# Second attention of a two-layer block: maxima over two PSUM banks at once, exponentials one bank at a time

## What is computed

```python
x = x + _L0_xattn_ref(_layernorm(x), ...)       # one head, 256 wide
x = x + _L0_ffn_ref(_layernorm(x), ...)         # 16 routed experts (top 2), 2 shared
x = x + _L1_xattn_ref(_layernorm(x), ctx, ...)  # 16 heads of 16, 4 key heads, over the 256 channels
x = x + _L1_ffn_ref(_layernorm(x), ...)         # ternary weights, 1024 wide
```

```python
q = q * cos + _rotate_half(q) * sin
k = k * cos + _rotate_half(k) * sin
k = jnp.repeat(k, 4, axis=1); v = jnp.repeat(v, 4, axis=1)
scores = jnp.einsum('bhqd,bhkd->bhqk', q, k) * scale
attn = jax.nn.softmax(scores, axis=-1)
out = jnp.einsum('bhqk,bhkd->bhqd', attn, v)
```

## Time and profile before

| | us |
|---|---|
| median of 3 runs | 815.56 (814.92 to 822.73) |
| the profiled execution, its own time | 824.98 |
| its span, first to last instruction | 823.2 |
| TensorE busy | 569.1 (69% of the span) |
| VectorE busy | 465.4 (57%) |
| ScalarE busy | 328.3 (40%) |
| GpSimd busy | 255.4 (31%) |
| maxima, 256 of 128x512 | 163.7 |
| exponentials, 128 of 128x1024 | 128.2 |

### The profile page before, as it was taken

How to read it: one execution, slowest core, us unless ns; L and a number is a source line. 1 busy time by engine, 2 the same in 40 slices (tenths; PEclk the granted TensorE clock), 3 DMA queues, 4 the chain that set the end, 5 groups by cost and what they waited for, 6 DMA issues and landing times. The chain is left out here.

```text
span 823.2 us, 11743 instructions
## 1 busy us (share of the span) xinstructions
PE 569.1 (69%) x4241; PEld 330.9 (40%) x4241; DVE 465.4 (57%) x1011; ACT 328.3 (40%) x488; POOL 255.4 (31%) x312
## 2 busy tenths in 40 slices
PE   3797907784882976633256877768876887776977
PEld 1575704674651756632022223223432342222444
DVE  2347660747831677752585686746766765660332
ACT  1113117455310656420023443524564546555523
POOL 2003125555374000035546122454323230000513
PEclk9898957986965989885557567879898998787979
DMA  9932082133124578522605210451115210101100
GB/s 259 299 109 87 26 268 73 36 77 106 39 103 127 130 194 199 122 89 30 118 1 117 53 31 22 91 106 17 39 29 115 39 41 2 31 6 26 29 26 26
DMA packets 97012, 68.73 MB, mean 83 GB/s; under 512 B 44265, under 2 KB 91003, under 8 KB 95995
## 3 DMA queue, kind: packets, MB, share of 16 engines
q1 hardware_dynamic: 91403, 56.18, 28.3%
q0 software_dynamic: 3504, 11.54, 4.8%
q10 hardware_dynamic: 2048, 0.27, 0.2%
HBM read 31.00 MB, written 24.38 MB: 67 GB/s over the span
## 5 line engine op out<-in xcount | busy, mean ns | idle before, releaser
L1773 DVE TENSOR_REDUCE M<-ps 128x2 f32<-128x512 f32 x256 | 163.7, 682 | 83.6 <-PE ps L1069 83.2
L1006 ACT ACTIVATE RW<-ps 128x1024 f32<-128x1024 f32 x128 | 128.2, 1024 | 138.8 <-PE ps L1069 126.4
L1069 PE MATMUL ps<-RS 128*128 128x128 f16 (+3 forms) x912 | 95.1, 270 | 40.9 <-DVE RS L1667 16.5
L1069 PEld LDWEIGHTS ps<-RS 128*128 128x128 f16 (+1 forms) x912 | 83.1, 130 | 53.1 <-DVE RS L1667 18.5
L1069 PE MATMUL ps<-RW,Vs 128*32 128x256 f32 x1024 | 89.8, 482 | 10.5 <-ACT wqkvo L1018 9.4
L1069 PE MATMUL ps<-RS,RW 48*128 48x256 bf16 (+1 forms) x448 | 58.6, 315 | 17.5 <-DVE M L1773 14.1
L1069 PE MATMUL ps<-tmp,xrow 48*128 48x256 bf16 x256 | 31.8, 334 | 40.9 <-DVE M L1773 25.5
L890 POOL TENSOR_TENSOR RS<-RS,RW 128x512 f16<-128x512 f32 x32 | 36.6, 1155 | 68.7 <-ACT RW L1054 68.7
L1069 PE MATMUL ps<-RS,wqkvo 128*128 128x512 f32 x64 | 36.5, 728 | 23.5 <-ACT RS L907 23.5
L1069 PE MATMUL ps<-RW,RS 50*128 50x512 bf16 (+1 forms) x224 | 45.0, 405 | 11.0 <-DMA RW<-mlo 8.9
L1069 PEld LDWEIGHTS ps<-RW,Vs 128*32 128x32 f32 x1024 | 31.1, 128 | 49.1 <-issue 24.5
(11 more groups left out here) (220 smaller groups left out, 964.3 us busy)
## 6 DMA issues: line engine op xcount, KB each, us to landing
sorted_scratch<-zero SPq DMA_DIRECT2D x1, 6144.0 KB, 19.9
expert_scratch<-RS SPq DMA_DIRECT2D x24, 256.0 KB, 2.7
RW<-in_wg SPq DMA_DIRECT2D x6, 384.0 KB, 6.2
RW<-in_wu SPq DMA_DIRECT2D x6, 384.0 KB, 6.6
RW<-in_w SPq DMA_DIRECT2D x3, 768.0 KB, 7.3
q_scratch<-RS SPq DMA_DIRECT2D x12, 192.0 KB, 2.7
acc<-in_x SPq DMA_DIRECT2D x4, 512.0 KB, 7.6
RS<-in_ctxT SPq DMA_DIRECT2D x8, 256.0 KB, 4.1
```

What stands on the lines that cost most here:

```text
L1006: act.activation(PT[:, k, :, :].rearrange("p i k -> p (i k)"), tile("st", n, 2), ACT.Exp, scale=float(HD) ** -0.5)\
L1069: return pe.matmul(out, lhsT, rhs, start=first, stop=last)
L1773: dve.tensor_reduce(M[:, 2 * p + kv // 2, at:at + 2], tile("smax", 2 * n + i).rearrange("p (a b) -> p a b", a=2), AX.X, ALU.max).then_inc( ...
```

## The change

The ring `max` gets a fourth bank, and a `smax` tile is now the two banks of a whole piece: four matmuls write it, one semaphore tells it full, and one reduction takes the maxima of both samples (1024 columns, four results a partition). `q1`, `mt` and `o1` now also take two banks of this ring, though they fill one at most. The ring `st` has three banks, and a `st` tile is one bank: two tiles a piece, each with its own wait for room, its own signal and its own exponential of 512 columns. `xt4`, `up4`, `gate4` and `down4` stay at one bank each, in a ring of three. The other lines follow the new counts.

```diff
-RINGS = {"main": (0, 1, 2, 3, 4, 5, 6), "max": (0, 1, 2), "st": (3, 4, 5, 6), "pv": (7,)}
+RINGS = {"main": (0, 1, 2, 3, 4, 5, 6), "max": (0, 1, 2, 3), "st": (4, 5, 6), "pv": (7,)}
...
     if what == "q1":
-        return [("q1", n, "max", 1, 2)]
+        return [("q1", n, "max", 2, 2)]
     if what == "mt":
-        return [("mt", n, "max", 1, 2)]
+        return [("mt", n, "max", 2, 2)]
     if what == "max":
-        return [("smax", m, "max", 1, 1) for m in two]
+        return [("smax", n, "max", 2, 1)]
     if what == "st":
-        return [("st", n, "st", 2, 1)]
+        return [("st", m, "st", 1, 1) for m in two]
...
     if what == "o1":
-        return [("o1", n, "max", 1, 1)]
+        return [("o1", n, "max", 2, 1)]
...
             def st(n):
-                act.wait_ge(*full("st", n))
                 t, k = divmod(n, 4)
                 if t:
                     act.wait_ge(weighted, 2 * (t - 1) + k // 2 + 1)
-                act.activation(PT[:, k, :, :].rearrange("p i k -> p (i k)"), tile("st", n, 2), ACT.Exp, scale=float(HD) ** -0.5)\
-                    .then_inc(emptied["st"], 1)
+                for i in range(2):
+                    act.wait_ge(*full("st", 2 * n + i))
+                    act.activation(PT[:, k, i, :], tile("st", 2 * n + i), ACT.Exp, scale=float(HD) ** -0.5).then_inc(emptied["st"], 1)
...
-                for i in range(2):
-                    room("smax", 2 * n + i)
+                room("smax", n)
                 for qb in range(2):
                     for i in range(2):
                         rows48 = slice(64 * i, 64 * i + ROWS)
-                        last = mm(tile("smax", 2 * n + i)[:, qb * T:(qb + 1) * T],
+                        at = (2 * i + qb) * T
+                        last = mm(tile("smax", n, 2)[:, at:at + T],
                                   QS[g % 2][rows48, p, KV * kv + hh, qb * P:(qb + 1) * P], KS[g % 2][rows48, p, kv, :])
-                        if qb:
-                            done(last, "smax")
+                done(last, "smax")
...
-                room("st", n)
                 for i in range(2):
+                    room("st", 2 * n + i)
                     rows50 = slice(64 * i, 64 * i + ROWS + 2)
-                    last = mm(tile("st", n, 2)[:, i * 512:(i + 1) * 512], KS[g % 2][rows50, p, kv, kb * P:(kb + 1) * P],
+                    last = mm(tile("st", 2 * n + i), KS[g % 2][rows50, p, kv, kb * P:(kb + 1) * P],
                               QS[g % 2][rows50, p, KV * kv + 2 * hf:KV * kv + 2 * hf + 2, :].rearrange("r h k -> r (h k)"))
-                done(last, "st")
+                    done(last, "st")
...
-                for i in range(2):
-                    dve.wait_ge(*full("smax", 2 * n + i))
-                    at = 16 * i + 8 * (kv % 2) + 2 * hh
-                    dve.tensor_reduce(M[:, 2 * p + kv // 2, at:at + 2], tile("smax", 2 * n + i).rearrange("p (a b) -> p a b", a=2),
-                                      AX.X, ALU.max).then_inc(emptied["smax"], 1)
+                dve.wait_ge(*full("smax", n))
+                at = 8 * (kv % 2) + 2 * hh
+                dve.tensor_reduce(M[:, 2 * p + kv // 2, :].rearrange("p (i a) -> p i a", i=2)[:, :, at:at + 2],
+                                  tile("smax", n, 2).rearrange("p (i a b) -> p i a b", i=2, a=2), AX.X, ALU.max)\
+                    .then_inc(emptied["smax"], 1)
```

More of the change, by code:

```diff
@@ L650, in keys @@
                 if g >= 2:
-                    sp.wait_ge(*full("st", 4 * (SPG * (g - 1) - 1) + 3))
+                    sp.wait_ge(*full("st", 8 * (SPG * (g - 1) - 1) + 7))
                 else:
@@ L654, in keys @@
                 if g:
-                    sp.wait_ge(*full("smax", 64 * (g - 1)))
+                    sp.wait_ge(*full("smax", 32 * (g - 1)))
                 for i in range(2):
@@ L665, in q1 @@
                 if g >= 2:
-                    sp.wait_ge(*full("st", 4 * (SPG * (g - 1) - 1) + 3))
+                    sp.wait_ge(*full("st", 8 * (SPG * (g - 1) - 1) + 7))
                 if g:
-                    sp.wait_ge(*full("smax", 64 * (g - 1) + 32 * p))
+                    sp.wait_ge(*full("smax", 32 * (g - 1) + 16 * p))
                 if n == 0:
@@ L1306, in maxima @@
                         rows48 = slice(64 * i, 64 * i + ROWS)
-                        last = mm(tile("smax", 2 * n + i)[:, qb * T:(qb + 1) * T],
+                        at = (2 * i + qb) * T
+                        last = mm(tile("smax", n, 2)[:, at:at + T],
                                   QS[g % 2][rows48, p, KV * kv + hh, qb * P:(qb + 1) * P], KS[g % 2][rows48, p, kv, :])
-                        if qb:
-                            done(last, "smax")
+                done(last, "smax")
             def mt(n):
                 room("mt", n)
-                pe.wait_ge(*empty("smax", 16 * n + 15))
+                pe.wait_ge(*empty("smax", 8 * n + 7))
                 done(pe.transpose(tile("mt", n)[0:32, 0:P], M[:, n % 4, :], ident[:]), "mt")
@@ L1338, in pv @@
                     pe.wait_ge(*empty("v1", NG - 1))
-                pe.wait_ge(*empty("st", 4 * t + 2 * kb + 1))
+                pe.wait_ge(*empty("st", 8 * t + 4 * kb + 3))
                 for i in range(2):
```

## The result

The changed kernel takes 847.54 us (median of 4 runs, 842.13 to 854.63), the kernel before beside it 818.09 (4 runs): a ratio of 1.0361, 95% interval 1.0259 to 1.0462. It is slower, outside the forecast range. The profiled execution after took 844.96 us, its span is 843.2, its mean granted clock 0.809. Ratios and intervals here leave out executions over 1.5% above the fastest one of the same kernel, which matters most for the kernel before with its reciprocals ahead: there they rest on the fastest six of twelve.

The account below looks back on a forecast made before the run. From 396 us the kernel was taken as bound by who waits for whom and by TensorE's clock. Terms -3.3-1.7-3.0+4.8+5.1+1.0 = +2.9 us, or 0.35% more, gave 818.4 us from 815.56; range 806 to 832 us.

Parts of the forecast that it names:

- The maxima: 256 reductions of 512 columns become 128 of 1024, 1.21 us each (ends 1.02 and 1.36); TensorE's wait 39.6 to below 12 us.
- The plain pair: Two slots, one step of scores at a time: 0.18 us won each, 18 x 0.18 = -3.3; 4.1 or 2.6 us after.
- the q1 stretch: Pairs with a q1 projection, 12 of them: shorter reduction and part of a 0.19 wait, 12 x 0.14 = -1.7 us.
- the three items: The forecast gains: plain pairs -3.3, pairs with a q1 projection -1.7, VectorE's backlog elsewhere -3.0 us.
- the -8.0: Forecast gains together: -3.3 in plain pairs, -1.7 in q1 pairs, -3.0 where VectorE has a backlog, in us.
- The exponentials: 128 of 1024 columns become 256 of 512, 594 ns each; 0.07 us more per st, mostly beside idle time of ScalarE.
- The new wait: TensorE's matmuls waiting for the exponential: 20 to 35 us, most of them 0.5 to 0.7 us before a single st matmul.
- the 1.0 that I gave to it: Stacking DMAs issued by ScalarE behind three exponentials, each 0.07 us later, about 13 such waits: +1.0 us.
- the price of the steps with two steps of scores: Steps 17, 18, 25, 26 and last: fourth bank waits for first exponential, 6 x 0.8 = +4.8 us, ends 0 and 8.
- Rival C: TensorE's clock: new stalls make it fall in ten more pairs, +15 us on top, 833 us; chance 0.11.
- The experts' ring: up4 and gate4 in three banks, up4 waiting for the product of n-2: +5.1 us, ends 0 and 7.
- Rival B: Slower by the ring of three; freed maxima wait not on the path, another ends there: +12.4 us, 828 us; chance 0.24.

Follow-up runs that it names:

- the kernel before with its reciprocals ahead: Kernel before, reciprocals of steps 12 and 20 moved ahead of the same step's q1 eviction in the list: 813.81 us, ratio 0.9874.
- The half exponentials: Changed kernel, exponentials in steps 17, 18, 25, 26, 33 on 256 of 512 columns: 842.39 us, ratio 1.0261; same in kernel before: 820.86 us, 1.0012.

## Why the prediction was wrong

**The maxima** went as forecast in their sizes: 1216 ns for 1.21 us, a wait of 17.9 us (forecast: below 12). The plain pair did not: 4.19 us at half clock for the 4.1 forecast, so 0.12 won of 0.18, and 2.81 at full clock for 2.6, nothing won. I had left out that a torn pair of `st` matmuls staggers the maxima behind it. Nor did the q1 stretch win anything (39.7 us for 38.8). Still the stretch from step 2 to 10 took some 4 us less, also at the same clock. Which of the three items holds that isn't shown. What was missed besides is that these microseconds aren't kept: the output projection of step 22 waits for a chain of DMAs that ends at the same moment (7.00 us instead of 3.48), and with this chain moved the gain didn't appear either. Over the whole kernel the -8.0 came out at nothing (ratio 1.0002). The cost of splitting the exponentials in the plain steps may be part of that; no run has the new maxima without it. (Two numbers are slightly off and carry nothing: 18 x 0.18 is 3.2, and 1024 columns at 1.03 ns are 1.06 us, not 1.02.)

**The exponentials** took 603 ns for the 594 forecast. The new wait is 16.9 us (forecast: 20 to 35). Splitting them costs more than the 1.0 that I gave to it: with four banks kept, 1.06% (0.25 to 1.88), some 9 us. TensorE's waits for exponentials grew by 4.8 us in that kernel's trace; the rest I didn't settle.

**The failed step is the price of the steps with two steps of scores**: "eight of these have `pv` behind them ... 6 x 0.8 = +4.8. The ends are 0 ... and 10 x 0.8 = 8". Measured were 20 us (847.5 to 828.15). The mechanism is the one named there (the fourth bank waits for the first exponential), and at half clock the price of one slot is near too (0.92 us). Two things were wrong.

First the count: I counted steps of scores, ten, but each has two slots with adjacent `st`, 20 in all, 16 with `pv` ahead. 16 x 0.92 is 14.7 us. The upper end of 8 made the range too narrow by the same error.

Second, the sum put the clock at nothing, and 0.92 is a price between two slots at half clock. Of the twelve stretches from `pv` to `pv` in steps 17, 18, 25 and 26, only one was at half clock in both kernels (+0.92). Three were at full clock in both (+0.65, +0.25 and 0). Seven ran at full clock before and at half, wholly or in part, after: they hold +14.9 us. (The twelfth, partly at half clock before, has +0.22.) By the slots above, half clock adds 0.83 to 1.50 us to a slot (3.26 against 2.43, from 686.89 to 689.32, and 1.76, with the rings of before). Seven times that is my estimate of what the clock took: 6 to 10 of the 20 us. That the clock goes with the ring is shown by the variants (0.70 to 0.85 with the ring of three in these steps, 0.84 to 1.00 without). How the waits bring it down is not: the one of 1.21 us stands ahead of the fall in step 25, and no run takes that one alone away. The half exponentials left both the slots and the clock (0.805) nearly as they were.

Rival C named this, but its mark, a mean clock that moves by over 0.03, was no good measure. It stood at 0.809 after 0.811 in the profiled executions, where the early stretch rose and the later one fell. Over all executions it was 0.790 to 0.823 in the changed kernel and 0.813 to 0.843 in the kernel before beside the variants.

**The experts' ring** cost 8 us for 5.1 forecast: the mechanism right, the term too small, and its upper end of 7 too. The waits of the two for products grew from 4.6 to 9.3 us.

**Rival B** (828, the ring of three) had the place right; only C's 833 was nearer. B's condition holds in part: at step 22 a chain of DMAs ends where the freed wait would have told. Its 12.4 us had the same count of ten slots. With 16 at 0.92, the 8 of the experts and 1.0 for the stacking it gives 0 - 1.7 + 14.7 + 8 + 1 = +22, or 840 us, reckoned from the 818.09 beside which 847.54 was measured. What is missing then is C's: the loss has a part of both rivals. The Trainium skill, "Perfetto Trace Analysis", Optimizing Scalar/DVE Operations, has it that smaller instructions may let work finish sooner where an engine isn't saturated but makes others wait. The runs don't bear it out: here ScalarE was busy for 40% of the span, and the split exponentials made the kernel 1.06% slower with every bank kept.

## What to carry to other kernels

A ring of buffers is sized in the units in which it is released: three half tiles behind a producer that writes four in a row stall it by one consumer's latency each time, and that stall recurs at every place where two producers are adjacent, so count these places in the list of work, not in the loop that generates it. Read the clock stretch by stretch and not as a mean: a price taken between two slots at one clock misses what the clock itself takes. Look at which wait ends last after the gain: some 4 us won early were gone behind a chain of DMAs that another queue's order fixed. Moving that chain by one place didn't bring them back, but it made the kernel before 0.6% faster by the medians. Two matmuls on different rows of the array overlap, so read a group's busy time beside its count and mean, not its mean alone.

## What the runs showed of the hardware that I had not expected

- Two matmuls of 50 rows on different partitions, each 0.47 us long, together cover 0.46 us on average when issued back to back (58.7 us for 128 pairs), and 0.64 in the changed kernel, where the second often has to wait (82.2).
- A store of 32 KB took 5.1 us to land in the kernel before and 6.9 where it was issued 1.4 us earlier, behind the same projection's DMAs: it landed at the same moment.
- The same slot of matmuls took 1.76 us at a granted clock of 1.00 and, in the other kernel, 4.18 at 0.50, of which 0.92 belongs to the kernel. In the changed kernel the fall from 1.00 to 0.50 came behind a wait of TensorE of 1.21 us.
- Executions of one kernel in one set of runs spread with the granted clock: the kernel before with the reciprocals ahead took 800.79 us at 0.838 and 824.44 at 0.807.
